# Two projections of a mixed attention and expert kernel: their inputs mixed once on ScalarE and VectorE instead of in the weights on TensorE

## The chip, the cores and the metric

One core of one Trainium2 chip runs the whole program. The metric is the device time of one execution in microseconds. Inside a core TensorE (PE), VectorE (DVE), ScalarE (ACT) and GpSimd (POOL) each run their own instruction list in order, and SyncE (SP) issues plain DMAs; they meet only at semaphores.

## The reference

x is 16 sequences of 512 tokens with 128 channels. After a layer norm, one branch is a recurrent attention with chunks of 32 tokens, the other a mixture of experts (8 experts, two per token, plus 8 small shared ones). The output is x + attention(x) * silu(experts(x)).

```python
xx = jnp.concatenate([jnp.zeros_like(x[:, :1]), x[:, :-1]], axis=1) - x
xk = x + xx * time_maa_k
xv = x + xx * time_maa_v
xr = x + xx * time_maa_r
r = split(proj(xr, Wr, br))
k = split(proj(xk, Wk, bk))
v = split(proj(xv, Wv, bv))
y, state = _wkv_chunked(r, k, v, time_decay, time_faaaa)
out = proj(y, Wo, bo)
...
routed = jnp.einsum('te,etd->td', gates, out_e)
alpha * shared + (1.0 - alpha) * routed
```

So each projection reads a mix of a token with the token in front of it: x*(1-m) + previous*m, with one m per channel.

## The kernel before

Values in float32 are held as a sum of two float16 numbers (high and low), and a product of two such values is three matmuls: high by high, high by low, low by high. The normed x lies transposed (channels on partitions) in `xh` and `xl`, with two zero columns ahead of each sequence, so that a slice shifted by one column is the previous token.

The program has four stages. First the norm, the transposes and the routing logits. Then a long run of expert work, which is 62 *units* cut in 206 *steps*: 12 shared units ahead of the sorted tokens (steps 0 to 47), then routed units with 4 shared ones mixed in. A wide unit (a shared one, or 512 sorted tokens) has 4 steps, a narrow one (256 sorted tokens) has 2. Steps 48 to 51 are two narrow units, 52 to 167 wide ones, 168 to 205 narrow ones. Last comes the recurrence over 16 pieces u, which this text calls the end stage.

One step i is a chain over the engines:

- PE, `pe_up(i)`: six 128x512 matmuls (twelve half ones for a narrow unit) into two of four PSUM banks; it waits for `gated` of step i-2. Then, in some steps, `pe_sorted` transposes a gathered block of 256 tokens, and `pe_down(i - 3)` makes the 12 small matmuls of an earlier step (LAG is 3; the profile's lines L1575 to L1577).
- ACT, `act_up(i)`, L781: silu of the first bank.
- DVE, `dve_up(i)`, L1218: its product with the second bank, called the gate here.
- ACT, `act_split(i)`, L785: the high half of that product.
- DVE, `dve_split(i)`, L1222: the low half. `pe_down(i)` needs both.

On DVE the list is gate(i), [the low half of a sorted block, L1211], low(i), [other work], gate(i+1). On ACT it is silu(i), [sorted block, L777], [a part, L817], high(i), [a copy out of PSUM when a unit ends, L805 or L807], silu(i+1). For wide units that copy falls on steps whose number leaves 2 when divided by 4, as every second sorted block does.

Between the steps r and k are projected in 32 *parts* of 512 tokens, one every 4 steps from step 75 (`PART_STEP`) to step 199. `pe_part` (L1596) stands at the end of step 75 + 4n: the mix is folded in the weights, W*(1-m) against x and W*m against the previous token, so a part is two times three matmuls of 512 columns. `act_part` adds the bias one step later (L817), `dve_part` makes the decayed copy two steps later (L1232), and SP stores both in DRAM. Parts 0 to 15 are r, 16 to 31 are k.

POOL gathers the sorted tokens (`pool_sorted`, L634, two indirect DMAs for each of 71 blocks, into `srows`, a ring of `NXB` blocks) and scatters the results (`pool_scatter`, L644, two for each block). Its list after the first seven blocks is strictly gather q, scatter q - 7, and a scatter waits for `y_out` of the block's unit. The end stage starts when all scatters have landed.

DVE also makes masks and weights for the end stage at ten even steps from `LATE_STEP` on, between gate and low half.

## Time and profile before

| what | value |
|---|---|
| median of the runs, us | 722.61 |
| lowest of the runs, us | 722.04 |
| span of the profiled execution, us | 719.3 |
| time around the span (median less span), us | 3.3 |
| silu of step 0, of step 74, of step 202, at us | 42.8, 229.4, 538.4 |
| first gather issued, at us | 154.7 |
| last scatter issued, at us | 554.0 |

The profiled execution's own total is not recorded apart from its span; the 3.3 us beside it are the median less the span, and they are added to every span below. Stage times are read from where the silu of a step starts. A length in the timeline is that of one instruction with its latency: on DVE and ACT the next one starts a little before the end of the one in front of it.

### The profile page before, as it was taken

To read this page: it belongs to the slowest core of one execution; us is meant where nothing else is said; L and a number is where in the kernel's file an instruction comes from. 1 tells how busy PE (TensorE), PEld (TensorE's weight loads), DVE (VectorE), ACT (ScalarE), POOL (GpSimd) and SP (SyncE) were. 2 spreads that over 40 slices of the span, in tenths; PEclk is the share of its full clock that TensorE was granted. 3 is DMA by queue.
4 is the path that set the end of the run, shared out by engine and by line. 5 is a ranking of instruction groups with operands and counts; after the bars stand their busy time and mean duration, and the time that the engine had idled before them with its cause. 6 is when DMAs were issued, how large, how long until landed. Compare 5 with 4: busy or idle time off the path is not lost.

```text
span 719.3 us, 22370 instructions
## 1 busy us (share of the span) xinstructions
PE 654.1 (91%) x8536; PEld 452.1 (63%) x8536; DVE 555.4 (77%) x1058; ACT 494.9 (69%) x1008; POOL 478.9 (67%) x519
## 2 busy tenths in 40 slices
PE   2787897978999999999999999999997899999993
PEld 1544565646665665566666666878886676777772
DVE  5989986877667886667766676667664899999996
ACT  4864798857665656666666666666665788888872
POOL 4844321244777777777777777767778487888873
PEclk9999999999999999999999999999999999999997
DMA  9931111111111323433323334333362767777762
GB/s 243 299 95 45 45 61 46 45 51 36 48 49 49 108 91 108 137 108 108 110 92 109 106 106 139 110 101 108 97 103 93 237 179 230 216 229 222 233 176 59
DMA packets 88616, 86.75 MB, mean 121 GB/s; under 512 B 11394, under 2 KB 65284, under 8 KB 88516
## 3 DMA queue, kind: packets, MB, share of 16 engines
q1 hardware_dynamic: 79428, 66.70, 29.8%
q0 software_dynamic: 9088, 18.63, 9.6%
q8 instruction: 73, 1.20, 0.7%
q14 instruction: 27, 0.22, 0.1%
HBM read 50.82 MB, written 34.47 MB: 119 GB/s over the span
## 4 chain that ended last, share of the span: by engine, by line
PE 53%; DVE 13%; ACT 12%; POOL 11%; issue 7%; DMA 3%; SPq 0%; POOLq 0%; DVEq 0%; ACTq 0%
PE banks L1556 7%; PE banks L1558 7%; PE banks L1557 7%; PE banks L1596 5%; DVE hidden L1218 4%; POOL expert_rows L644 4%; PE banks L1576 4%; PE banks L1577 4%; PE banks L1575 4%; POOL srows L634 3%; ACT hidden L785 3%; PE banks L1621 3%; PE banks L1693 3%; PE banks L1672 3%; ACT rows L823 2%
## 5 line engine op out<-in xcount | busy, mean ns | idle before, releaser
L785 ACT CAST hidden<-hidden 128x512 f16<-128x512 f32 x206 | 127.1, 617 | 135.5 <-DVE hidden L1218 135.4
L634 POOL DMA_INDIRECT srows<-normed_rows,source x142 | 149.7, 1054 | 60.4 <-issue 40.2
L1222 DVE TENSOR_TENSOR hidden<-hidden 128x512 f16<-128x512 f32 x180 | 124.4, 691 | 83.9 <-ACT hidden L785 83.0
L1218 DVE TENSOR_TENSOR hidden<-hidden,banks 128x512 f32<-128x512 f32 x206 | 140.8, 684 | 44.0 <-ACT hidden L781 38.2
L1575 PE MATMUL banks<-wwords,hidden 128*128 (+1 forms) x824 | 148.8, 219 | 1.5 <-DVE hidden L1222 1.1
L1576 PE MATMUL banks<-wwords,hidden 128*128 (+1 forms) x824 | 148.6, 219 | 0.0
L1577 PE MATMUL banks<-wwords,hidden 128*128 (+1 forms) x824 | 148.6, 219 | 0.0
L781 ACT ACTIVATE hidden<-banks 128x512 f32<-128x512 f32 x206 | 122.7, 596 | 28.1 <-PE banks L1558 27.8
L1556 PE MATMUL banks<-sx,wwords 128*128 128x512 f16 (+1 forms) x368 | 121.5, 330 | 3.2 <-DVE wwords L1013 2.7
L1558 PE MATMUL banks<-sx,wwords 128*128 128x512 f16 (+1 forms) x368 | 121.6, 330 | 0.0
L1557 PE MATMUL banks<-sx,wwords 128*128 128x512 f16 (+1 forms) x368 | 121.5, 330 | 0.0
L644 POOL DMA_INDIRECT expert_rows<-ybuf,dest x72 | 77.2, 1072 | 22.8 <-issue 19.8
L1575 PEld LDWEIGHTS banks<-wwords,hidden 128*128 128x128 f16 x824 | 80.6, 98 | 12.4 <-issue 2.0
L644 POOL DMA_INDIRECT expert_rows<-rows,dest x70 | 72.8, 1040 | 23.1 <-issue 20.1
L1576 PEld LDWEIGHTS banks<-wwords,hidden 128*128 128x128 f16 x824 | 80.6, 98 | 11.3
L624 POOL TENSOR_TENSOR hidden<-hidden 128x512 f16<-128x512 f32 x26 | 33.6, 1294 | 76.8 <-ACT hidden L785 76.8
L1303 DVE TENSOR_TENSOR wwords<-banks,wmat 128x1024 f32<-128x1024 f32 x64 | 75.3, 1217 | 10.9 <-PE banks L1672 10.5
L1577 PEld LDWEIGHTS banks<-wwords,hidden 128*128 128x128 f16 x824 | 80.6, 98 | 0.0
L1556 PE MATMUL banks<-xh,wwords 128*128 128x512 f16 x128 | 49.2, 385 | 19.1 <-DVE hidden L1218 18.7
L1321 DVE SCALAR_TENSOR_TENSOR hidden<-banks,cst,hidden 128x256 f32<-128x256 f32 x128 | 61.5, 481 | 3.8 <-ACT hidden L849 0.7
L1558 PEld LDWEIGHTS banks<-sx,wwords 128*128 x368 | 36.0, 98 | 25.6
L1557 PE MATMUL banks<-xl,wwords 128*128 128x512 f16 x128 | 49.0, 383 | 0.0
(218 smaller groups left out, 1429.7 us busy)
## 6 DMA issues: line engine op xcount, KB each, us to landing
rows<-x SPq DMA_DIRECT2D x32, 256.0 KB, 4.9
rows<-expert_rows SPq DMA_DIRECT2D x32, 256.0 KB, 3.6
normed_rows<-rows SPq DMA_DIRECT2D x16, 256.0 KB, 3.9
r_rows<-rows SPq DMA_DIRECT2D x16, 256.0 KB, 2.1
rd_rows<-rows SPq DMA_DIRECT2D x16, 256.0 KB, 2.2
stage<-r_rows SPq DMA_DIRECT2D x16, 256.0 KB, 4.0
k_rows<-rows SPq DMA_DIRECT2D x16, 256.0 KB, 2.2
kd_rows<-rows SPq DMA_DIRECT2D x16, 256.0 KB, 2.2
```

The lines of the kernel that those rows point to most:

```text
L634: G.indirect_dma_start(srows[:, q % NXB, t, :], None, rows_in, bass.IndirectOffsetOnAxis(source[:, at:at + 1], 0)).then_inc(sem[f"s_in{q % ...
L644: G.indirect_dma_start(rows_out, bass.IndirectOffsetOnAxis(dest[:, at:at + 1], 0), ring_of(q)[:, t, :], None).then_inc(sem[f"y_stored{q % ...
L781: A.activation(sg[:, i % 2, :], psum[2 * (i % 2)][:, :], ACT.Silu, scale=1.0 / SW).then_inc(sem["silu"], 1)
L785: A.copy(guh[:, i % 4, :], gu[:, i % 2, :]).then_inc(sem["gu_hi"], 1)
L1218: V.tensor_tensor(gu[:, i % 2, :], sg[:, i % 2, :], psum[2 * (i % 2) + 1][:, :], ALU.mult).then_inc(sem["gated"], 1)
L1222: V.tensor_tensor(gul[:, i % 4, :], gu[:, i % 2, :], guh[:, i % 4, :], ALU.subtract).then_inc(sem["gu_lo"], 1)
L1556: T.matmul(o, a, mh, start=True, stop=False)
L1557: T.matmul(o, a, ml, start=False, stop=False)
L1558: k = T.matmul(o, b, mh, start=False, stop=True)
L1575: T.matmul(o, guh[:, i % 4, s], a, start=(j == 0 and n == 0), stop=False)
L1576: T.matmul(o, guh[:, i % 4, s], b, start=False, stop=False)
L1577: k = T.matmul(o, gul[:, i % 4, s], a, start=False, stop=last)
```

## The change

`act_previous` (ACT, two steps ahead of the part) writes previous*m into `mixed`, `dve_mix` (DVE, the same step) adds x*(1-m), `act_mix_high` and `dve_mix_low` (one step ahead of the part) split it in two float16 tiles, and `pe_part` makes three products of 512 columns with unmixed weights, after a wait for `mix_lo`. `dve_xsum` (DVE, three steps ahead of every second part) adds `xh` and `xl` for 129 columns of four sequences; it serves the r part and the k part of the same tokens, which are now neighbours (n even is r, n odd is k). `mixed`, `mix_hi` and `mix_lo` are single tiles in `stage`. The work at `LATE_STEP` moves from steps 72 to 90 to steps 50 to 68, and the ring `srows` has five blocks. The weights of v and of the output keep their form, with new numbers. POOL's clearing of the first state now waits for the last part, and SP loads the first pieces of k at the last-but-one part.

```diff
@@ -152,7 +152,7 @@
-        NXB = 3
+        NXB = 5
         srows = sb("srows", [P, NXB, TPU, P])
...
@@ -245,6 +246,10 @@
         ypair = take([P, 2, TPU, P])
+
+        take = carve(stage[:, :, :].rearrange("p a b -> p (a b)"))
+        mixed = take([P, 512])
+        mix_hi, mix_lo = [take([P, 512], F16) for i in range(2)]
...
@@ -411,8 +416,8 @@
-        LATE_STEP = 72
-        R_PARTS, PARTS = NA, 2 * NA
+        LATE_STEP = 50
+        PARTS = 2 * NA
         PART_STEP = 75
...
@@ -645,6 +650,7 @@
             def pool_state0():
+                G.wait_ge(sem["part"], PARTS)
                 G.wait_ge(sem["w_hi"], 3 * (EXPERTS + 1))
...
@@ -815,6 +821,22 @@
+
+            def act_previous(n):
+                u, proj = divmod(n, 2)
+                A.wait_ge(sem["xsum"], u + 1)
+                if n == 0:
+                    A.wait_ge(sem["w_lo"], 3 * (EXPERTS + 1))
+                    A.wait_ge(sem["mix_in"], 48)
+                else:
+                    A.wait_ge(sem["mix_lo"], n)
+                A.mul(mixed[:, :].rearrange("p (b i) -> p b i", b=4), xsum[:, :, 0:P], mx[:, proj:proj + 1]).then_inc(sem["mix_prev"], 1)
+
+            def act_mix_high(n):
+                A.wait_ge(sem["mixed"], n + 1)
+                if n >= 1:
+                    A.wait_ge(sem["part"], n)
+                A.copy(mix_hi[:, :], mixed[:, :]).then_inc(sem["mix_hi"], 1)
...
@@ -913,6 +935,10 @@
                     act_split(i)
+                    if part_at(i + 2) is not None:
+                        act_previous(part_at(i + 2))
+                    if part_at(i + 1) is not None:
+                        act_mix_high(part_at(i + 1))
                     if y is not None and filled:
...
@@ -1222,16 +1247,39 @@
-                w = wb if n < R_PARTS else wk
+                w = (wb, wk)[n % 2]
-                    V.wait_ge(sem["mixes"], 7)
+                    V.wait_ge(sem["mixes"], 6)
+
+            def dve_xsum(u):
+                tt, g = where(u)
+                if u == 0:
+                    V.wait_ge(sem["x_lo"], nb)
+                    V.wait_ge(sem["zero_cols"], 2 * nb)
+                h, l = [a[:, 4 * g * XS:4 * (g + 1) * XS].rearrange("p (b s) -> p b s", s=XS)[:, :, 1 + tt * P:2 + (tt + 1) * P]
+                        for a in (xh, xl)]
+                V.tensor_tensor(xsum[:, :, :], h, l, ALU.add).then_inc(sem["xsum"], 1)
+
+            def dve_mix(n):
+                proj = n % 2
+                V.wait_ge(sem["mix_prev"], n + 1)
+                if n == 0:
+                    V.wait_ge(sem["mixes"], 1)
+                m = mixed[:, :].rearrange("p (b i) -> p b i", b=4)
+                V.scalar_tensor_tensor(m, xsum[:, :, 1:P + 1], omx[:, proj:proj + 1], m, ALU.mult, ALU.add).then_inc(sem["mixed"], 1)
+
+            def dve_mix_low(n):
+                V.wait_ge(sem["mix_hi"], n + 1)
+                if n >= 1:
+                    V.wait_ge(sem["part"], n)
+                V.tensor_tensor(mix_lo[:, :], mixed[:, :], mix_hi[:, :], ALU.subtract).then_inc(sem["mix_lo"], 1)
...
@@ -1249,32 +1297,34 @@
                     V.wait_ge(sem["mixes"], 1)
-                    V.tensor_scalar(ws32[:, 6, :], w32[:, 3, :], SW, None, ALU.mult).then_inc(sem["aconst"], 1)
-                V.tensor_scalar(ws32[:, i, :], w32[:, i, :], omx[:, i:i + 1], SW, ALU.mult, ALU.mult).then_inc(sem["aconst"], 1)
-                V.tensor_scalar(ws32[:, 3 + i, :], w32[:, i, :], mx[:, i:i + 1], SW, ALU.mult, ALU.mult).then_inc(sem["aconst"], 1)
+                    V.tensor_scalar(ws32[:, 1, :], w32[:, 1, :], SW, None, ALU.mult).then_inc(sem["aconst"], 1)
+                    V.tensor_scalar(ws32[:, 4, :], w32[:, 3, :], SW, None, ALU.mult).then_inc(sem["aconst"], 1)
+                else:
+                    V.tensor_scalar(ws32[:, 2, :], w32[:, 2, :], omx[:, 2:3], SW, ALU.mult, ALU.mult).then_inc(sem["aconst"], 1)
+                    V.tensor_scalar(ws32[:, 3, :], w32[:, 2, :], mx[:, 2:3], SW, ALU.mult, ALU.mult).then_inc(sem["aconst"], 1)
-                V.wait_ge(sem["aconst"], 8 + 2 * step)
-                for some in (slice(1, 3), slice(4, 7)):
-                    if step == 0:
-                        V.tensor_copy(wph[:, some, :], ws32[:, some, :]).then_inc(sem["aconst"], 1)
-                    else:
-                        V.tensor_tensor(wpl[:, some, :], ws32[:, some, :], wph[:, some, :], ALU.subtract).then_inc(sem["aconst"], 1)
+                V.wait_ge(sem["aconst"], 7 + step)
+                some = slice(1, 5)
+                if step == 0:
+                    V.tensor_copy(wph[:, some, :], ws32[:, some, :]).then_inc(sem["aconst"], 1)
+                else:
+                    V.tensor_tensor(wpl[:, some, :], ws32[:, some, :], wph[:, some, :], ALU.subtract).then_inc(sem["aconst"], 1)
...
@@ -1579,23 +1635,17 @@
             def pe_part(n):
-                u, proj = n % R_PARTS, n // R_PARTS
-                tt, g = where(u)
+                proj = n % 2
+                T.wait_ge(sem["mix_lo"], n + 1)
                 if n == 0:
-                    T.wait_ge(sem["mixes"], 6)
-                    T.wait_ge(sem["zero_cols"], 2 * nb)
                     T.wait_ge(sem["source"], 1)
                     T.wait_ge(sem["part_out"], n)
-                if n == R_PARTS:
-                    T.wait_ge(sem["aconst"], 12)
-                i = 0
-                for shift in range(2):
-                    mh, ml = [cols(t, g, shift)(tt) for t in (xh, xl)]
-                    for a, m in ((wph, mh), (wph, ml), (wpl, mh)):
-                        j = T.matmul(psum[7], a[:, 3 * shift + proj, :], m, start=(i == 0), stop=(i == 5))
-                        i += 1
-                j.then_inc(sem["part"], 1)
+                if n == 1:
+                    T.wait_ge(sem["aconst"], 9)
+                T.matmul(psum[7], wph[:, proj, :], mix_hi[:, :], start=True, stop=False)
+                T.matmul(psum[7], wph[:, proj, :], mix_lo[:, :], start=False, stop=False)
+                T.matmul(psum[7], wpl[:, proj, :], mix_hi[:, :], start=False, stop=True).then_inc(sem["part"], 1)
...
@@ -1618,7 +1668,7 @@
                         for a, m in ((ch, wph), (ch, wpl), (cl, wph)):
-                            j = T.matmul(o, a, m[:, 3 * shift + 2, :], start=False, stop=(n == 5))
+                            j = T.matmul(o, a, m[:, 2 + shift, :], start=False, stop=(n == 5))
                             n += 1
```

On DVE, in the third stage over the four steps from one whose number leaves 2 when divided by 4 (step 134 and its like): before,

```order
L1218 TENSOR_TENSOR hidden<-hidden,banks 128x512 [waits gu_lo,silu]
L1211 TENSOR_TENSOR sx<-banks,sx 128x256 [waits s_hi]
L1222 TENSOR_TENSOR hidden<-hidden 128x512 [waits gu_hi]
L1218 TENSOR_TENSOR hidden<-hidden,banks 128x512 [waits gu_lo,silu]
L1222 TENSOR_TENSOR hidden<-hidden 128x512 [waits gu_hi]
L1218 TENSOR_TENSOR hidden<-hidden,banks 128x512 [waits gu_lo,silu]
L1222 TENSOR_TENSOR hidden<-hidden 128x512 [waits gu_hi]
L1218 TENSOR_TENSOR hidden<-hidden,banks 128x512 [waits gu_lo,silu]
L1222 TENSOR_TENSOR hidden<-hidden 128x512 [waits gu_hi]
L1232 TENSOR_TENSOR rows<-rows,wb 128x512 [waits part_stored1,part_out]
```

and with the change (L1243 is the gate, L1247 the low half, L1282 `dve_mix_low`, L1268 `dve_xsum`, L1276 `dve_mix`, with `dve_part` next in the list):

```order
L1243 TENSOR_TENSOR hidden<-hidden,banks 128x512 [waits gu_lo,silu]
L1236 TENSOR_TENSOR sx<-banks,sx 128x256 [waits s_hi]
L1247 TENSOR_TENSOR hidden<-hidden 128x512 [waits gu_hi]
L1282 TENSOR_TENSOR stage<-stage 128x512 [waits part,mix_hi]
L1243 TENSOR_TENSOR hidden<-hidden,banks 128x512 [waits gu_lo,silu]
L1247 TENSOR_TENSOR hidden<-hidden 128x512 [waits gu_hi]
L1243 TENSOR_TENSOR hidden<-hidden,banks 128x512 [waits gu_lo,silu]
L1247 TENSOR_TENSOR hidden<-hidden 128x512 [waits gu_hi]
L1268 TENSOR_TENSOR xsum<-xh,xl 128x516
L1243 TENSOR_TENSOR hidden<-hidden,banks 128x512 [waits gu_lo,silu]
L1247 TENSOR_TENSOR hidden<-hidden 128x512 [waits gu_hi]
L1276 SCALAR_TENSOR_TENSOR stage<-xsum,omx,stage 128x512 [waits mix_prev]
```

The three new instructions all stand behind a low half and ahead of the next gate.

On ACT, two steps ahead of a part and one step ahead: before,

```order
L785 CAST hidden<-hidden 128x512 [waits gated]
L781 ACTIVATE hidden<-banks 128x512 [waits up]
L777 CAST sx<-banks 128x256 [waits s_flipped]
L785 CAST hidden<-hidden 128x512 [waits gated]
L805 COPY rows<-banks 128x512 [waits y_stored3,y_stored2,down]
L781 ACTIVATE hidden<-banks 128x512 [waits up]
L785 CAST hidden<-hidden 128x512 [waits gated]
```

and with the change (L787 is the silu, L791 the high half, L811 the copy of a finished unit, L833 `act_previous`, L839 `act_mix_high`):

```order
L791 CAST hidden<-hidden 128x512 [waits gated]
L833 ACTIVATE stage<-xsum,mx 128x512 [waits mix_lo,xsum]
L787 ACTIVATE hidden<-banks 128x512 [waits up]
L783 CAST sx<-banks 128x256 [waits s_flipped]
L791 CAST hidden<-hidden 128x512 [waits gated]
L839 CAST stage<-stage 128x512 [waits part,mixed]
L811 COPY rows<-banks 128x512 [waits y_stored3,y_stored2,down]
L787 ACTIVATE hidden<-banks 128x512 [waits up]
L791 CAST hidden<-hidden 128x512 [waits gated]
```

Both new instructions stand behind a high half and ahead of the next silu, the second of them also ahead of the copy.

On PE, at the end of a part's step and the start of the next: before,

```order
L1576 MATMUL banks<-wwords,hidden 128x128
L1577 MATMUL banks<-wwords,hidden 128x128
L1596 MATMUL banks<-xh,wph 128x512 [waits part_out]
L1596 MATMUL banks<-xl,wph 128x512
L1596 MATMUL banks<-xh,wpl 128x512
L1596 MATMUL banks<-xh,wph 128x512
L1596 MATMUL banks<-xl,wph 128x512
L1596 MATMUL banks<-xh,wpl 128x512
L1556 ISA [waits gated,s_lo]
L1556 MATMUL banks<-sx,wwords 128x512
```

and with the change (L1646 to L1648 are `pe_part`):

```order
L1632 MATMUL banks<-wwords,hidden 128x128
L1633 MATMUL banks<-wwords,hidden 128x128
L1646 MATMUL banks<-stage,wph 128x512 [waits part_out,mix_lo]
L1647 MATMUL banks<-stage,wph 128x512
L1648 MATMUL banks<-stage,wpl 128x512
L1612 ISA [waits gated,s_lo]
L1612 MATMUL banks<-sx,wwords 128x512
```

The part has half its products, and its first one now waits for DVE's `mix_lo`; the up matmuls of the next step are queued behind it.

## Rows read from the trace of the kernel before

**Rows 1.** Part 1 of the page: busy time of each engine.

```profile
PE 654.1 (91%) x8536; PEld 452.1 (63%) x8536; DVE 555.4 (77%) x1058; ACT 494.9 (69%) x1008; POOL 478.9 (67%) x519
```

**Rows 2.** Windows view (columns: stretch, busy per engine, PEclk, DMA share, GB/s).

```profile
213.00:290.00 77.00, 74.36 (x642) 47.01 (x641) 57.81 (x104) 48.00 (x92) 60.13 (x56) 1.00 0.27 86
290.00:540.00 250.00, 249.08 (x2334) 177.02 (x2332) 171.22 (x280) 161.87 (x313) 189.71 (x182) 1.00 0.36 110
```

**Rows 3.** Chain that ended last, by line, in the stretch 340 to 380 us.

```profile
by line: PE banks L1556 17.8%; PE banks L1557 17.8%; PE banks L1558 17.3%; PE banks L1596 16.5%; PE banks L1577 8.9%; PE banks L1576 8.9%; PE banks L1575 8.9%; PE banks L1509 4.4%
```

**Rows 4.** Groups by line, POOL, 290 to 540 us (busy, mean ns, idle before, releasers).

```profile
L634 POOL DMA_INDIRECT srows<-normed_rows,source x89 | 92.1, 1035 | 30.3 <-issue 25.9 <-PE banks L1509 4.4
L644 POOL DMA_INDIRECT expert_rows<-ybuf,dest x47 | 49.9, 1062 | 15.2 <-issue 12.8 <-ACT ybuf L805 1.2 <-ACT rows L807 0.9
L644 POOL DMA_INDIRECT expert_rows<-rows,dest x46 | 48.3, 1050 | 14.9 <-issue 13.1 <-ACT rows L805 1.2 <-ACT ybuf L805 0.3
```

**Rows 5.** Timeline of POOL: the longest wait after 290 us, the next gather.

```profile
471.16 1.31 POOL L634 DMA_INDIRECT srows<-normed_rows,source  x1 [3.53 <-PE banks L1509]
472.77 0.96 POOL L634 DMA_INDIRECT srows<-normed_rows,source  x1 [0.30 <-issue]
```

**Rows 6.** Timeline of DVE over one period (start, length, line, idle before).

```profile
367.16 0.68 DVE L1218 TENSOR_TENSOR hidden<-hidden,banks 128x512 f32<-128x512 f32 x1
...
368.52 0.69 DVE L1222 TENSOR_TENSOR hidden<-hidden 128x512 f16<-128x512 f32 x1 [0.35 <-ACT hidden L785]
369.51 0.69 DVE L1218 TENSOR_TENSOR hidden<-hidden,banks 128x512 f32<-128x512 f32 x1 [0.29 <-ACT hidden L781]
...
372.01 0.69 DVE L1218 TENSOR_TENSOR hidden<-hidden,banks 128x512 f32<-128x512 f32 x1 [0.44 <-ACT hidden L781]
...
374.19 0.69 DVE L1218 TENSOR_TENSOR hidden<-hidden,banks 128x512 f32<-128x512 f32 x1
375.56 0.69 DVE L1222 TENSOR_TENSOR hidden<-hidden 128x512 f16<-128x512 f32 x1 [0.69 <-ACT hidden L785]
376.17 0.69 DVE L1232 TENSOR_TENSOR rows<-rows,wb 128x512 f32<-128x512 f32 x1
376.77 0.68 DVE L1218 TENSOR_TENSOR hidden<-hidden,banks 128x512 f32<-128x512 f32 x1
```

**Rows 7.** Timeline of ACT, step 130 to 131.

```profile
367.87 0.62 ACT L785 CAST hidden<-hidden 128x512 f16<-128x512 f32 x1 [1.10 <-DVE hidden L1218]
368.40 0.58 ACT L805 COPY rows<-banks 128x512 f32<-128x512 f32 x1
368.87 0.60 ACT L781 ACTIVATE hidden<-banks 128x512 f32<-128x512 f32 x1
```

**Rows 8.** Timeline of PE: first product of part 14, last of up(132).

```profile
368.57 0.38 PE L1596 MATMUL banks<-xh,wph 128*128 128x512 f16 x1
...
370.96 0.38 PE L1558 MATMUL banks<-sx,wwords 128*128 128x512 f16 x1
```

**Rows 9.** Timeline of DVE around the first mask of the third stage.

```profile
225.82 0.68 DVE L1218 TENSOR_TENSOR hidden<-hidden,banks 128x512 f32<-128x512 f32 x1
226.41 1.22 DVE L1240 TENSOR_TENSOR wmat<-wmat,cst 128x1024 f32<-128x1024 f32 x1
227.55 0.68 DVE L1222 TENSOR_TENSOR hidden<-hidden 128x512 f16<-128x512 f32 x1
```

**Rows 10.** Timeline of ACT: the silu of step 74 and of step 202.

```profile
229.39 0.59 ACT L781 ACTIVATE hidden<-banks 128x512 f32<-128x512 f32 x1
...
538.41 0.60 ACT L781 ACTIVATE hidden<-banks 128x512 f32<-128x512 f32 x1
```

**Rows 11.** Timeline of ACT and POOL: last copy of expert rows, last scatter.

```profile
548.88 0.37 ACT L807 COPY rows<-banks 128x256 f32<-128x256 f32 x1 [1.54 <-PE banks L1577]
...
554.04 0.97 POOL L644 DMA_INDIRECT expert_rows<-rows,dest  x1 [0.31 <-issue]
```

**Rows 12.** Windows view, a stretch of the first eleven units.

```profile
100.00:120.00 20.00, 16.38 (x155) 10.52 (x153) 13.83 (x22) 18.85 (x32) 4.50 (x4) 0.96 0.14 47
```

60 lines of the change are left out of this document (33 added, 27 removed).

## The prediction

> **What bounds the kernel now.** I read the page's busy shares first: PE is busy 91% of the span and no other engine over 77% [rows 1], which suggests PE, but is a mean over four stages. So next the windows of the routed stretch. From 213 to 290 us PE is busy 74.4 of 77 us and from 290 to 540 us 249.1 of 250 at full clock [rows 2]. The chain of waits agrees: between 340 and 380 us it consists of PE lines alone, and 16.5% of it is the part, L1596 [rows 3]. There a matmul taken away is time taken away, as long as nobody else is close behind.
>
> Two others are. POOL shows 189.7 us busy in the same 250 us [rows 2], but each of its 182 issues is followed by some 0.30 us that the profile calls issue; what it truly waited for is 4.4 us on PE and 1.2 + 0.9 + 1.2 + 0.3 = 3.6 us on ACT [rows 4], and the largest of these is a single wait of 3.53 us [rows 5]. So POOL could run this stretch at most 8.0 us faster.
>
> The other is the loop between DVE and ACT, and it shows only in the timeline. In step 130 the gate starts at 367.16, the low half at 368.52; in step 133 they are at 374.19 and 375.56 [rows 6]. The 1.37 us between them are the gate, then ACT's high half, which starts 0.71 after the gate (367.87) [rows 7]. DVE stands idle for half of it, but its list is in order, so nothing behind the low half can use that hole. Behind a low half the next instruction starts 0.61 later (375.56 to 376.17) and one more costs 0.60 (376.17 to 376.77) [rows 6]. The shortest step of this loop is therefore 1.36 + 0.61 = 1.97 us. The period of four steps 130 to 133 took 376.77 - 367.16 = 9.61 us; the loop alone would need 4 x 1.97, 0.60 for the decayed copy and 0.38 for step 130, where the copy of a finished unit holds the silu (gate 131 at 369.51 and not at 369.13; ACT's starts are 367.87, 368.40, 368.87) [rows 6, 7]: 8.9 us. It has 0.7 us of slack in 9.6, and that is all the room there is for the new work.
>
> **PE's side.** The last product of up(132) starts 2.39 us after the first of part 14, eleven products later: 0.217 us each [rows 8]. Three fewer save 0.65 us a part, 32 x 0.65 = 20.8 us in all if PE stays last.
>
> **DVE's and ACT's side.** The new instructions have no row of their own. The nearest for the three on DVE is the decayed copy, of the same 128x512 in float32: 0.60 to the next start and 0.69 long [rows 6]. A wide instruction there can cost nothing if it falls in the hole and 0.69 if nothing overlaps; I take 0.61, since all three stand behind a low half. I walk the period again from gate 130 at 367.16.
>
> Step 130 (one ahead of the part). Low half 368.52, `dve_mix_low` 369.13. Its input, ACT's `act_mix_high`, starts 0.53 behind the high half, at 368.40, and is like it 0.62 us long [rows 7], so it is there by 369.02. `dve_mix_low` ends at 369.82. The part on PE started at 368.57 [rows 8]; it now waits until about 369.92, with 0.10 for the semaphore and the weights (between 0 and 0.2). The copy of the finished unit moves to 368.93, silu 131 to 369.40, gate 131, 0.64 behind its silu [rows 6, 7], to 370.04.
>
> Step 131 and the start of 132. Queued behind the waiting part on PE are the up matmuls of step 132; behind those wait ACT's silu and DVE's gate. From the part's first product to gate 132 it is 372.01 - 368.57 = 3.44 us now [rows 6, 8], less 0.65 with three products: gate 132 at 369.92 + 2.79 = 372.71. DVE itself would be free at 370.04 + 1.97 = 372.01. The two gates are 5.55 us apart and were 4.85.
>
> Step 132. It took 2.18 us (372.01 to 374.19) [rows 6]. DVE's `dve_xsum`, every second time, makes it 1.97 + 0.61 = 2.58; the mean is 2.38.
>
> Step 133 (two ahead of the next part). It took 2.58 [rows 6]. `act_previous` starts 0.53 behind the high half, 1.24 after the gate, and is done, at ACT's lengths of 0.60 to 0.62 [rows 7], about when DVE comes to `dve_mix`, 1.97 after the gate. That adds 0.61: 3.19.
>
> Sum: 5.55 + 2.38 + 3.19 = **11.12 us a period** against 9.61, 1.5 us more although PE does less. Between the silus of steps 74 and 202 there are 32 periods in 538.41 - 229.39 = 309.0 us [rows 10], 9.66 each. Now 32 x 11.12 = 355.8: **46.8 us more**. POOL needs (309.0 - 8.0)/32 = 9.4 us a period on average and stays ahead of this loop.
>
> On the price of one more instruction the Trainium skill, "VectorE: DVE Perf Modes", section "The DRAIN you can't avoid", speaks otherwise: the next instruction starts only when the pipeline is empty. By it each of the 2.5 new ones in a period would cost its full 0.69 and not 0.61, some 6 us more in the sum. The trace shows 0.60 between the starts of an instruction of 0.69 and the next [rows 6], so the row is kept.
>
> **The smaller parts.** The late work moves to steps 50 to 68, into DVE's hole there. A mask makes the way from gate to low half 227.55 - 225.82 = 1.73 instead of 1.37, 0.36 more [rows 9]; beside a sorted block it also loses the room of that. For ten such steps I bound it by 0 (POOL's list may be what is late there) and 10 x 0.5 = 5, and take 2. The gain where the work leaves is nothing, since POOL held that stretch too. The ring of five: a gather no longer waits for the third block before it, but the scatter next in POOL's list waits for its unit all the same, so I take 0, between 0 and the 4.4 us of rows 4 as a gain. At the end of the stretch POOL was late: ACT's last copy of expert rows started at 548.88, the last scatter at 554.04 [rows 11]. With POOL caught up only two scatters come behind that copy, at about 549.3 and 550.6, 3.4 us sooner; I take 2, as the first loads of the end stage hide some of it. POOL's new wait for the last part is long over by then, and SP issues its later loads of k ten steps before the end stage; both cost nothing, and a few us if that cover were gone. The weights of v and the output keep their number of products.
>
> Together 719.3 + 46.8 + 2 - 2 = 766.1 us of span, and with the 3.3 us around it **769.4 us**.
>
> **Rivals.** *The part does not wait.* If PE comes late enough, or DVE early enough, that `mix_lo` is there, gate 132 is at 372.01, the period 4.85 + 2.38 + 3.19 = 10.42, and the whole 26 us slower: 748.6. For it speaks only that my 0.7 us is a difference of two estimates. *POOL becomes the bound.* If the new DVE and ACT work finds room in their waits (DVE is busy 171 of 250 us, ACT 162 [rows 2]), PE saves 0.65 a part and POOL stops the gain at 8.0 us: 714.6, no change that can be told. The in-order lists speak against it. *PE's saving is whole.* As before, and the longer ring lets POOL run ahead: 722.6 - 20.8 = 701.8, faster. It needs DVE's loop to grow by less than 0.05 us a period (8.9 + x below 9.61 - 0.65), while 2.5 new instructions stand in it, and POOL to do in 12.8 us less than its issues allow. *The clock falls.* From 100 to 120 us PE was busy 16.4 of 20 us, having waited for DVE and ACT, and the granted clock was 0.96 on average, so between the levels of 2.4 and 1.2 GHz [rows 12]; with the change PE waits about 2 us in each 11. If 8% of the time were at the lower level, the nine products of a period's late path (2.0 us) would take 0.16 longer: 5 us, 774.5. The Trainium skill, "TensorE: Matmul & The Clock Gate", section "The HAM clock gate", says that the gate follows how busy the array has been of late, which agrees in direction.
>
> **How the numbers follow.** A difference of 2%, 14.5 us, is about what a measurement of this kernel tells from none. I give my forecast 0.62, the part that does not wait 0.13, the clock or otherwise longer instructions 0.10, POOL as bound 0.12, the whole saving 0.03. Leaving out the last two and a few hundredths of the tails, the range is 741 to 780. Faster by over 2%: 0.04; within 2%: 0.13; slower: 0.83.
>
> **What would show it.** In the timeline of the changed kernel: gates of a period 5.5, 2.0 or 2.6, and 3.2 us apart; each part's first product right behind the end of `dve_mix_low`, with PE idle ahead of it for over 1 us; POOL's waits for PE and ACT grown from 8 to some 50 us; PE no longer the engine of the chain from 230 to 540 us, but DVE and ACT with it. I would be wrong if DVE ran any new instruction in its hole, if a new one took well under 0.6 us, or if PE stayed over 95% busy in that stretch.

## The result

| what | before | after |
|---|---|---|
| median of the runs, us | 722.33 | 794.80 |
| range of the runs beside it, us | 720.6 to 722.6 | 792.6 to 796.2 |
| span of the profiled execution, us | 719.3 | 790.6 |
| silu of step 0, of step 74, of step 202, at us | 42.8, 229.4, 538.4 | 44.6, 233.6, 610.7 |
| mean granted TensorE clock | 0.988 | 0.954 |

The changed kernel takes 1.1005 times as long, with a 95% interval of 1.0977 to 1.1033: 72 us more for three matmuls less in each of 32 parts. One execution of the kernel before took 2308 us and is left out of the range. The forecast was 769.4 us in a range of 741 to 780. The direction and the longer loop were right; the size was not, because the sum put the price of TensorE's clock at nothing.

Where the time went can be read from four marks. Step 0 starts 1.8 us later. That is no part of the change: the same code up to there starts step 0 at 43.0 in the first experiment below. From step 0 to step 74 it is 189.0 us and was 186.6, 2.4 more. From step 74 to step 202 it is 377.2 us and was 309.0 [rows 10]: **68.2 us more**. From step 202 to the end it is 179.9 and was 180.9. So nearly everything lies in the stretch with the parts.

Part 1 of the page after, which answers to [rows 1]:

```profile
PE 662.0 (84%) x8440; PEld 456.0 (58%) x8440; DVE 604.5 (76%) x1134; ACT 526.3 (67%) x1072; POOL 474.5 (60%) x519
```

96 matmuls are gone, and still PE is busy 7.9 us longer. A matmul count that falls while the busy time rises means that single matmuls took longer, and that points at the clock. The windows of the changed kernel, as in [rows 2] (columns: stretch, its length, busy time of PE, PEld, DVE, ACT, POOL, granted clock, DMA share, GB/s):

```profile
213.00:290.00 77.00, 64.99 (x567) 41.25 (x565) 57.11 (x97) 48.85 (x94) 55.55 (x54) 1.00 0.24 77
290.00:540.00 250.00, 206.10 (x1712) 135.06 (x1711) 169.69 (x277) 151.12 (x288) 154.91 (x152) 0.93 0.28 88
```

PE was busy 249.1 of 250 us here and is now busy 206.1, for fewer steps, and the granted clock has gone from 1.00 to 0.93. Who waits for whom stands in the view of waits (who waits for whom: us in total, times, longest):

```profile
PE banks L1646 <- DVE stage L1282: 66.2, 32, 2.7
DVE hidden L1243 <- ACT hidden L787: 65.3, 82, 4.3
ACT hidden L787 <- PE banks L1614: 54.9, 57, 2.6
```

All 32 parts wait for `dve_mix_low` (L1282), 2.07 us each on average. L1243 is the gate now, L787 the silu, L791 the high half, L1247 the low half, L1612 to L1614 the up matmuls. The second and third row are one and the same delay handed on: the up matmuls stand behind the waiting part, ACT waits for them, and DVE for ACT. POOL, by line from 290 to 540 us, answers to [rows 4]:

```profile
L639 POOL DMA_INDIRECT srows<-normed_rows,source x76 | 77.0, 1014 | 25.9 <-issue 20.4 <-PE banks L1565 5.5
L649 POOL DMA_INDIRECT expert_rows<-rows,dest x40 | 41.8, 1044 | 36.3 <-ACT rows L811 26.5 <-issue 9.7
L649 POOL DMA_INDIRECT expert_rows<-ybuf,dest x36 | 36.8, 1023 | 33.2 <-ACT ybuf L811 24.2 <-issue 8.9
```

It truly waited 5.5 + 26.5 + 24.2 = 56.2 us here and 8.0 before, so it does not bound the changed kernel. The chain of 340 to 380 us, PE lines alone before [rows 3], now runs over every engine of the loop (its end is cut by the view itself):

```profile
by line: issue 14.0%; ACT hidden L791 12.1%; DVE hidden L1243 9.4%; PE banks L1614 7.6%; PE banks L1613 7.3%; DVE stage L1282 6.9%; PE banks L1612 6.5%; DVE hidden L1247 5.7%; DVE rows L1257 5.1%; PE banks L1646 3.9%; DVE xsum L1268 3.4%; A
```

**One period at full clock.** The timeline of DVE, steps 134 to 137 (start, length, line, idle before):

```profile
409.76 0.68 DVE L1243 TENSOR_TENSOR hidden<-hidden,banks 128x512 f32<-128x512 f32 x1
410.36 0.41 DVE L1236 TENSOR_TENSOR sx<-banks,sx 128x256 f16<-128x256 f32 x1
411.12 0.69 DVE L1247 TENSOR_TENSOR hidden<-hidden 128x512 f16<-128x512 f32 x1 [0.35 <-ACT hidden L791]
411.73 0.68 DVE L1282 TENSOR_TENSOR stage<-stage 128x512 f16<-128x512 f32 x1
412.63 0.69 DVE L1243 TENSOR_TENSOR hidden<-hidden,banks 128x512 f32<-128x512 f32 x1 [0.21 <-ACT hidden L787]
414.00 0.69 DVE L1247 TENSOR_TENSOR hidden<-hidden 128x512 f16<-128x512 f32 x1 [0.69 <-ACT hidden L791]
415.26 0.69 DVE L1243 TENSOR_TENSOR hidden<-hidden,banks 128x512 f32<-128x512 f32 x1 [0.57 <-ACT hidden L787]
...
417.24 0.69 DVE L1268 TENSOR_TENSOR xsum<-xh,xl 128x516 f32<-128x516 f16 x1
417.85 0.68 DVE L1243 TENSOR_TENSOR hidden<-hidden,banks 128x512 f32<-128x512 f32 x1
419.21 0.69 DVE L1247 TENSOR_TENSOR hidden<-hidden 128x512 f16<-128x512 f32 x1 [0.69 <-ACT hidden L791]
419.83 0.75 DVE L1276 SCALAR_TENSOR_TENSOR stage<-xsum,omx,stage 128x512 f32<-128x512 f32 x1
420.50 0.68 DVE L1257 TENSOR_TENSOR rows<-rows,wk 128x512 f32<-128x512 f32 x1
421.11 0.68 DVE L1243 TENSOR_TENSOR hidden<-hidden,banks 128x512 f32<-128x512 f32 x1
```

The gates are 415.26 - 409.76 = 5.50, then 2.59 and 3.26 us apart, 11.35 together; this is a period with `dve_xsum`, for which the prediction's terms are 5.55 + 2.58 + 3.19 = 11.32. The three new instructions stand where the prediction put them, and DVE's hole of 0.69 between gate and low half is still empty.

**One period with a fallen clock.** The period before, 397.14 to 409.76, took 12.62 though it has no `dve_xsum`. The timeline of PE shows why. The last down matmul ahead of the part started at 397.41:

```profile
399.85 0.39 PE L1646 MATMUL banks<-stage,wph 128*128 128x512 f16 x1 [2.23 <-DVE stage L1282]
400.08 0.38 PE L1647 MATMUL banks<-stage,wph 128*128 128x512 f16 x1
400.30 0.38 PE L1648 MATMUL banks<-stage,wpl 128*128 128x512 f16 x1
400.51 0.44 PE L1612 MATMUL banks<-sx,wwords 128*128 128x512 f16 x1
400.75 0.63 PE L1613 MATMUL banks<-sx,wwords 128*128 128x512 f16 x1
401.17 0.63 PE L1614 MATMUL banks<-sx,wwords 128*128 128x512 f16 x1
401.60 0.63 PE L1612 MATMUL banks<-sx,wwords 128*128 128x512 f16 x1
402.03 0.63 PE L1613 MATMUL banks<-sx,wwords 128*128 128x512 f16 x1
```

The part's products start 0.22 us apart, as at 2.4 GHz. After an idle of 2.23 us and three to four products the pitch becomes 0.43: the level of 1.2 GHz, until about 404.1. The windows view has half the clock there:

```profile
400.80:404.00 3.20, 3.20 (x15) 1.84 (x14) 0.94 (x2) 1.42 (x4) 2.34 (x3) 0.50 0.15 46
```

These are the up matmuls that the whole loop is waiting for. What one such spell costs is read from pairs of periods, each with one `dve_xsum`. The first products of the parts start at 237.08, 259.38, 281.67, 304.00, every second one, and these pairs are 22.3 us long; from there they start at 327.96, 351.92, 375.89, 399.85, 423.82, 447.79, 471.76, 23.96 us long: 1.65 us for a spell. From 304 on, every second part has a spell, 13 in all: 13 x 1.65 = 21.5 us. Over time the spell begins earlier against its part: in the sixth product from the part's first at 304.00, in the fourth at 399.85, the third at 519.75, the first at 591.74. At 495.74, 543.70, 567.73 and 591.74 it falls on the half-size products of narrow steps, 0.21 us apart in place of 0.11. (The narrow steps are 164 to 171 and 176 to 205, with a wide shared unit at 172 to 175, and not 168 to 205 as said ahead of the prediction; the pairs there are 24.0 us long, and 22.3 with the clock held up in the first experiment below, as the wide ones are.) The six parts ahead of 304 have none, with the same idle of 1.8 and 2.2 us ahead of them.

### The profile page after: what moved, and what is told of

Read it like the earlier page. It is cut to its first block, busy times and chain, and to the rows that moved or that the text cites. A ratio compares the mean times of both kernels' runs of the same rounds, so it can differ in the third digit from the quotient of the medians.

```text
span 790.6 us, 22444 instructions
## 1 busy us (share of the span) xinstructions
PE 662.0 (84%) x8440; PEld 456.0 (58%) x8440; DVE 604.5 (76%) x1134; ACT 526.3 (67%) x1072; POOL 474.5 (60%) x519
## 4 chain that ended last, share of the span: by engine, by line
DVE 30%; PE 30%; ACT 21%; issue 13%; POOL 3%; DMA 1%; DVEq 0%; SPq 0%; POOLq 0%; ACTq 0%
DVE hidden L1243 11%; ACT hidden L791 10%; DVE hidden L1247 4%; ACT hidden L787 4%; PE banks L1614 3%; PE banks L1613 3%; PE banks L1612 3%; PE banks L1671 3%; DVE stage L1282 3%; DVE rows L1257 3%; PE banks L1722 3%; PE banks L1743 2%; ACT rows L845 2%; PE banks L1646 2%; POOL hidden L676 2%
## 5 line engine op out<-in xcount | busy, mean ns | idle before, releaser
L791 ACT CAST hidden<-hidden 128x512 f16<-128x512 f32 x206 | 127.1, 617 | 151.9 <-DVE hidden L1243 151.9
L1243 DVE TENSOR_TENSOR hidden<-hidden,banks 128x512 f32<-128x512 f32 x206 | 140.7, 683 | 66.5 <-ACT hidden L787 65.3
L1247 DVE TENSOR_TENSOR hidden<-hidden 128x512 f16<-128x512 f32 x180 | 124.5, 692 | 85.0 <-ACT hidden L791 84.2
L639 POOL DMA_INDIRECT srows<-normed_rows,source x142 | 147.5, 1038 | 54.2 <-issue 38.1
L787 ACT ACTIVATE hidden<-banks 128x512 f32<-128x512 f32 x206 | 121.9, 592 | 55.0 <-PE banks L1614 54.9
L1631 PE MATMUL banks<-wwords,hidden 128*128 (+1 forms) x824 | 152.6, 222 | 1.5 <-DVE hidden L1247 1.1
L1632 PE MATMUL banks<-wwords,hidden 128*128 (+1 forms) x824 | 152.0, 222 | 0.0
L1633 PE MATMUL banks<-wwords,hidden 128*128 (+1 forms) x824 | 151.6, 222 | 0.0
L1612 PE MATMUL banks<-sx,wwords 128*128 128x512 f16 (+1 forms) x368 | 126.1, 343 | 4.4 <-DVE wwords L1038 2.7
L1614 PE MATMUL banks<-sx,wwords 128*128 128x512 f16 (+1 forms) x368 | 126.8, 345 | 0.0
L1613 PE MATMUL banks<-sx,wwords 128*128 128x512 f16 (+1 forms) x368 | 126.6, 344 | 0.0
L649 POOL DMA_INDIRECT expert_rows<-ybuf,dest x72 | 74.5, 1034 | 66.9 <-ACT ybuf L811 25.2
L1631 PEld LDWEIGHTS banks<-wwords,hidden 128*128 128x128 f16 x824 | 82.3, 100 | 12.6 <-issue 2.2
L1632 PEld LDWEIGHTS banks<-wwords,hidden 128*128 128x128 f16 x824 | 82.1, 100 | 11.9 <-issue 0.3
L1633 PEld LDWEIGHTS banks<-wwords,hidden 128*128 128x128 f16 x824 | 82.0, 99 | 0.0
L1646 PE MATMUL banks<-stage,wph 128*128 128x512 f16 x32 | 12.7, 395 | 66.2 <-DVE stage L1282 66.2
L1612 PE MATMUL banks<-xh,wwords 128*128 128x512 f16 x128 | 50.9, 398 | 18.7 <-DVE hidden L1243 18.3
L1614 PEld LDWEIGHTS banks<-sx,wwords 128*128 x368 | 37.4, 102 | 27.7 <-issue 2.2
```

What stands on the lines that cost most here:

```text
L639: G.indirect_dma_start(srows[:, q % NXB, t, :], None, rows_in, bass.IndirectOffsetOnAxis(source[:, at:at + 1], 0)).then_inc(sem[f"s_in{q % ...
L649: G.indirect_dma_start(rows_out, bass.IndirectOffsetOnAxis(dest[:, at:at + 1], 0), ring_of(q)[:, t, :], None).then_inc(sem[f"y_stored{q % ...
L787: A.activation(sg[:, i % 2, :], psum[2 * (i % 2)][:, :], ACT.Silu, scale=1.0 / SW).then_inc(sem["silu"], 1)
L791: A.copy(guh[:, i % 4, :], gu[:, i % 2, :]).then_inc(sem["gu_hi"], 1)
L1243: V.tensor_tensor(gu[:, i % 2, :], sg[:, i % 2, :], psum[2 * (i % 2) + 1][:, :], ALU.mult).then_inc(sem["gated"], 1)
L1247: V.tensor_tensor(gul[:, i % 4, :], gu[:, i % 2, :], guh[:, i % 4, :], ALU.subtract).then_inc(sem["gu_lo"], 1)
```

## The experiments

Each run stood beside runs of the kernel before on the same chip. Edits are against the changed kernel unless said otherwise.

### PE kept from idling: eight extra products

```diff
                 else:
                     T.wait_ge(sem["part_out"], n)
+                for j in range(8):
+                    T.matmul(psum[7], wph[:, 0, :], xh[:, j * XS + 2:j * XS + 2 + WIDE], start=(j == 0), stop=(j == 7))
+                T.wait_ge(sem["mix_lo"], n + 1)
```

The wait for `mix_lo`, first in `pe_part` until now, moves behind them; the part's own products overwrite the bank.

> The changed kernel, with eight extra products of 512 columns (8 x 0.217 = 1.74 us) on TensorE ahead of each part's wait for mix_lo. Their result is overwritten by the part. Theory (the wait on DVE's mix_lo costs twice, by itself and because TensorE's clock falls after it): the extra products fit in the wait of 1.8 to 2.7 us, the granted clock stays near 1.0 from 230 to 610 us, a period of four steps takes about 11.2 us and not 11.8, so 32 x 0.6 = 19 us less than the changed kernel: about 775 us. Rival (the clock is no cause, only the lists of DVE and ACT are): the same 794.8 us. Rival (TensorE's own work still bounds): 32 x 1.74 = 56 us more, 850 us.

Measured: 773.6 us (772.5 to 774.4), 1.071 times the kernel before (1.0685 to 1.0734). Doing 256 matmuls more made the kernel 21 us faster. The granted clock of 290 to 540 us is back at full:

```profile
290.00:540.00 250.00, 241.82 (x2031) 153.41 (x2029) 182.28 (x297) 161.68 (x309) 162.19 (x160) 1.00 0.30 93
```

The silus of steps 74 and 202 start here:

```profile
233.67 0.58 ACT L787 ACTIVATE hidden<-banks 128x512 f32<-128x512 f32 x1
...
589.35 0.60 ACT L787 ACTIVATE hidden<-banks 128x512 f32<-128x512 f32 x1
```

355.7 us or 11.11 a period. With the clock out of the way, the walk of the prediction (11.12, 355.8) holds, part's wait included. The whole is still 4.2 us above the forecast of 769.4; where these stand is told behind the experiments.

### Four extra products: busy share or idle stretch?

The same edit with 4 in place of 8. It leaves PE idle for part of the wait.

> e1_fill with four extra products (0.87 us) and not eight. TensorE still stands idle for 1.0 to 1.8 us ahead of each part. Theory (the clock falls after a long idle stretch, not because TensorE is less busy on the whole): the clock stays up in nearly all periods, about 774 us as with eight. Rival (it goes by the busy share alone): between the 795 us of the changed kernel and the 774 us of e1_fill, about 785 us.

Measured: 775.1 us (773.9 to 778.1), 1.0741 (1.0707 to 1.0776), so the same as with eight (1.0685 to 1.0734). One of its parts in the timeline of PE:

```profile
390.98 1.03 PE L1644 MATMUL banks<-xh,wph 128*128 128x512 f16 x4
393.37 0.39 PE L1648 MATMUL banks<-stage,wph 128*128 128x512 f16 x1 [1.36 <-DVE stage L1282]
393.59 0.38 PE L1649 MATMUL banks<-stage,wph 128*128 128x512 f16 x1
```

The idle time ahead of a part is 1.36 (three times 1.6 to 1.8) where it was 2.2 and 1.0 where it was 1.8, and no spell is left. It is enough to shorten the idle stretch; filling it brings nothing more. It does not tell idle stretch from busy share: four products also raise PE's busy time from 206.1 to 222.0 of the 250 us, and only the rival that the loss goes in proportion to the share (785) is ruled out.

### The same work one step earlier

```diff
-                    if part_at(i + 2) is not None:
-                        act_previous(part_at(i + 2))
-                    if part_at(i + 1) is not None:
-                        act_mix_high(part_at(i + 1))
+                    if part_at(i + 3) is not None:
+                        act_previous(part_at(i + 3))
+                    if part_at(i + 2) is not None:
+                        act_mix_high(part_at(i + 2))
```

and on DVE likewise `dve_xsum` at i + 4, `dve_mix` at i + 3, `dve_mix_low` at i + 2. The part finds `mix_lo` ready.

> The changed kernel, with the sum, the mix and the split made one step earlier against the part (four, three and two steps ahead, not three, two and one), at the same places behind a low half. Theory: the part no longer waits, the clock stays up, and what is left is DVE's in-order list: four shortest steps of 1.97, 0.38 for the copy, and 0.30 + 0.67 + 0.61 + 0.60 for sum, mix, low half and decayed copy, 10.4 us a period; 32 x (11.79 - 10.4) = 44 us less than the changed kernel: about 751 us. Rival (only the new instructions count, not the wait on the part): 795 us. Rival (only the wait counts): POOL is last, 714 us.

Measured: 746.6 us (746.4 to 747.6), 1.034 (1.0318 to 1.0362). Silu 74 starts at 232.91 and silu 202 at 563.36: 330.5 us, 10.33 a period. No row of waits for DVE stands ahead of a part any more:

```profile
337.24 0.38 PE L1646 MATMUL banks<-stage,wph 128*128 128x512 f16 x1
```

This is the first rival of the prediction (period 10.42, 748.6 us; by the rule of its main sum it would be 32 x 10.42 - 309.0 = 24.4 us more, 747.0) made to happen. Beside the run with eight extra products, the wait by itself, at full clock, is 773.6 - 746.6 = 27 us.

### The same work in the holes

On ACT the two instructions move from behind the high half to ahead of it, on DVE all of them, the decayed copy too, from behind the low half to between gate and low half.

```diff
+                if part_at(i + 7) is not None and part_at(i + 7) % 2 == 0:
+                    dve_xsum(part_at(i + 7) // 2)
+                if part_at(i + 4) is not None:
+                    dve_mix(part_at(i + 4))
+                if part_at(i + 2) is not None:
+                    dve_mix_low(part_at(i + 2))
+                if part_at(i - 3) is not None:
+                    dve_part(part_at(i - 3))
                 if not low_on_pool(i):
                     dve_split(i)
```

with the old places removed, ACT's at i + 4 and i + 2 ahead of `act_split`, and a wait of `dve_xsum` for the last reader of its tile.

> The changed kernel with the same instructions at other places of the lists: on ACT previous and high ahead of the high half of the step (four and two steps ahead of the part), on DVE mix and low of the mix ahead of the low half of the same steps, the sum seven steps ahead and the decayed copy three steps behind, also ahead of the low half. Theory (what costs is the place, behind a low half, not the instruction): the new work falls in the 0.76 us in which DVE waits for the high half, DVE's loop takes 4 x 1.97 + 0.38 + about 0.3 = 8.6 us a period, TensorE does not wait for mix_lo, and POOL is last: about 714 us. Rival (each of the new instructions costs its length wherever it stands): 750 us or more.

Measured: 726.4 us (721.5 to 728.0, 10 runs), 1.0046 (1.0024 to 1.0067). So 20 us of the 24 that the early version lost are recovered by the place; the forecast 714 was missed by 12. Two things moved with it: the lead over the part is one to three steps longer, which can bring little since no part of the early version waits, and the decayed copy, an old instruction of 0.60 us a period, left its place behind the low half too. What the new instructions alone would cost in the hole was not run. Silu 74 at 235.33, silu 202 at 541.97: 306.6 us, 9.58 a period with every new instruction in it. DVE's hole is used and costs nothing: with `dve_mix` (L1278) in it the low half starts 411.40 - 410.03 = 1.37 behind the gate, as without:

```profile
407.68 0.68 DVE L1243 TENSOR_TENSOR hidden<-hidden,banks 128x512 f32<-128x512 f32 x1
408.28 0.42 DVE L1236 TENSOR_TENSOR sx<-banks,sx 128x256 f16<-128x256 f32 x1
408.61 0.68 DVE L1257 TENSOR_TENSOR rows<-rows,wk 128x512 f32<-128x512 f32 x1
409.21 0.68 DVE L1247 TENSOR_TENSOR hidden<-hidden 128x512 f16<-128x512 f32 x1
410.03 0.69 DVE L1243 TENSOR_TENSOR hidden<-hidden,banks 128x512 f32<-128x512 f32 x1
410.64 0.75 DVE L1278 SCALAR_TENSOR_TENSOR stage<-xsum,omx,stage 128x512 f32<-128x512 f32 x1
411.40 0.69 DVE L1247 TENSOR_TENSOR hidden<-hidden 128x512 f16<-128x512 f32 x1
```

Only beside a sorted block does the low half slip, to 1.53 behind its gate (407.68 to 409.21). Why no gain is left is seen better with no mix at all.

### Three products and no mix at all

DVE's and ACT's new instructions are left out and the part multiplies x itself, so r and k are projections of x and not of the mix. It shows how much the saving on PE can bring in this kernel.

> The changed kernel with the mix left out altogether: three products of 512 columns of the unmixed tokens a part, no sum, mix or split on ACT and DVE, so r and k are projections of x alone. It measures TensorE's saving by itself. Theory: TensorE would save 32 x 0.65 = 20.8 us, but POOL's list has only some 8 us of slack: about 714 us. Rival (the saving is whole once the ring has five blocks): 702 us. Rival (the ring, the moved late work or the new order of r and k cost something by themselves): above 722 us.

Measured: 721.0 us (717.6 to 724.5, 9 runs), 0.998 (0.9956 to 1.0003): neither 714 nor 702. The chain of 290 to 540 us begins:

```profile
by line: POOL expert_rows L649 17.4%; POOL srows L639 15.5%; issue 13.3%; PE banks L1604 6.8%; PE banks L1602 6.8%; PE banks L1603 6.8%; DMA srows<-normed_rows,source 4.9%; DVE hidden L1239 3.7%; PE banks L1622 3.6%; PE banks L1621 3.6%; PE
```

POOL leads it, as the theory of POOL as bound says, but it gave back less than the 8.0 us. The timeline of POOL names the places where it waits for more than 0.5 us between its first gather and its last scatter, and those two:

```profile
156.77 1.36 POOL L639 DMA_INDIRECT srows<-normed_rows,source  x1 [5.73 <-DVE source L1195]
...
187.25 1.14 POOL L649 DMA_INDIRECT expert_rows<-ybuf,dest  x1 [4.88 <-ACT ybuf L813]
...
200.69 1.00 POOL L649 DMA_INDIRECT expert_rows<-rows,dest  x1 [2.54 <-ACT rows L811]
...
552.63 0.96 POOL L649 DMA_INDIRECT expert_rows<-rows,dest  x1 [0.30 <-issue]
```

(and two of 1.29 and 1.99 at 175.06 and 179.24). From 200.69 it never stops: 351.9 us to the last scatter. The kernel before, in the same view, has its last wait ahead of the parts at 197.52 and two more in the parts' stretch beside that of [rows 5]:

```profile
197.52 0.99 POOL L644 DMA_INDIRECT expert_rows<-rows,dest  x1 [1.18 <-ACT rows L805]
340.42 0.99 POOL L644 DMA_INDIRECT expert_rows<-ybuf,dest  x1 [1.18 <-ACT ybuf L805]
416.90 0.99 POOL L644 DMA_INDIRECT expert_rows<-rows,dest  x1 [1.18 <-ACT rows L805]
```

From 197.52 it took 554.04 - 197.52 = 356.5 us, with 1.18 + 1.18 + 3.53 = 5.9 us of waits in it. So 4.6 us were won behind that scatter, and it was issued 3.2 later: 2.1 because the whole program started later in this execution, 1.1 because the head of the list took longer. With the deeper ring POOL waits less for blocks there, and runs ahead to a scatter whose unit is not ready. The kernel before with the ring of five alone, its late work at step 72 as ever, has the same two waits:

```profile
186.18 1.05 POOL L644 DMA_INDIRECT expert_rows<-ybuf,dest  x1 [5.39 <-ACT ybuf L807]
...
198.85 0.99 POOL L644 DMA_INDIRECT expert_rows<-rows,dest  x1 [2.06 <-ACT rows L805]
```

and the changed kernel with a ring of three has only one of 1.18 there, as before the change. From first gather to last scatter the list takes 395.9 us with no mix, 400.1 with the mix in the holes, 399.4 before. Before, its 284 issues are 299.7 us long (1.06 each) with 80.1 of issue between them, 380 us, and 19.3 us of waits behind the first gather; with no mix the waits are 14.4, and the issues 1.4 longer. So what there was to win is small. That POOL is what holds the time is read from its timeline and the chain; no run made its list shorter by itself.

The profiled execution gained nothing of this in the end: its last scatter is 1.4 us earlier than before, and from there to the end it took 168.7 us and 165.3 before. That part of the program varies: it is 170.5 us in the trace of the kernel before with the ring of five, so no cause can be read from it.

### The ring, alone and undone

The kernel before with `NXB = 5`, and the changed kernel with `NXB = 3`.

> The kernel before with a ring of five blocks, on whichever chip the call falls. On a chip where the kernel before takes 722 us: theory, within 3 us of it; rival, 3 to 4% slower as on the two chips where the kernel before took 820 to 830 us.

> The changed kernel with NXB 3 in place of 5. Theory: POOL waits for 100 us in the changed kernel, its ring bounds nothing: within 3 us of the changed kernel's 795 us. Rival (the ring of five is part of the loss): faster by over 5 us.

Measured: 722.8 us, 1.0003 (0.9987 to 1.002), and 795.4 us, 1.1017 (1.0987 to 1.1047). The ring is neither part of the loss nor a gain: in the trace of the kernel before with five blocks POOL waited 3.9 us for blocks and 11.9 for units, with three 14.5 and 4.8.

### A longer lag for the scatters

The version with the work in the holes, with `LATE_STEP` 64 and scatter q - 9 in place of q - 7, so that POOL has gathers to issue while a unit is unfinished.

> The kernel of e9_lag9 (work in the holes, late work at step 64, scatter nine blocks behind the gather). Theory (POOL's list is last, 5 us of gathers moved into its first wait, late work off the first wide unit): 718 to 722 us where the kernel before takes 722 us and e4_holes 726. Rival: the 726 us of e4_holes.

Measured: 724.4 us (721.7 to 725.6, 10 runs), 1.0019 (1.0002 to 1.0037). Of the waits for units at the head of the list, 4.88 and 2.54 with q - 7, one of 1.18 is left. But the scatters to `expert_rows` from `ybuf` took 1.117 us each and 1.072 before, the gathers 1.075 and 1.054, and the list is 398.6 us long, as ever. Against the version with q - 7, which ran on another chip (1.0024 to 1.0067), the intervals overlap, so no gain is shown, and two things were changed at once. It is not better than the kernel before: the expectation was missed. On the chips where the kernel before takes 722 us, no version with the mix beat it.

### Two chips that tell little

The ring alone and three variants of the version in the holes (`LATE_STEP` 64; then scatter q - 8; then q - 9) first ran on another chip, and were repeated on a third.

> The kernel before with NXB 5 in place of 3 and nothing else. Theory: the second half of POOL's list is strictly gather, scatter, and a scatter waits for its unit, so a longer ring lets POOL ahead by two blocks once and then gives nothing: within 3 us of the 722.4 us of the kernel before. Rival (the ring was what held POOL): POOL's waits for transposes, 4.4 us after 290 us and 9.8 us before, go, and the time falls by 5 to 10 us.

> The kernel e4_holes with the late work at steps 64 to 82 in place of 50 to 68. In e4_holes POOL issues without a pause from 202.9 us (its scatter of the first wide unit, which waited 2.5 us for that unit) to 558 us. Theory: the late work on DVE at steps 50 to 58 delays that unit, and with it the whole list of POOL: 2 to 3.5 us less than e4_holes, about 723.5 us. Rival (its place does not matter, since POOL is last): 726.4 us.

> e7_late64 with scatter q - 8 and not q - 7 behind gather q: POOL issues one more block of gathers in the time in which it waits for the first units. Theory (POOL's list is what is last in the third stage): one block of gathers, 2 x 1.3 us, moves into that wait: 2.6 us less than e7_late64. Rival (POOL is last only because the units come at their pace): no difference, or more, since a copy out of PSUM waits longer for its place in the ring of four.

> The same with q - 9: two blocks of gathers in the wait. Theory: up to 2.6 us less than e8_lag8 as far as the ring of five has room; the ninth gather waits for the transpose of block 4, so it may be less. Rival: POOL's order comes to wait on TensorE and TensorE on POOL's scatters, and it is slower than e8_lag8.

And of the repetition:

> The kernel of e5_ring5 again (the kernel before with a ring of five blocks), since in that call the kernel before itself took 830 us, with pauses of up to 8 us on ACT and DVE that no engine ended. Theory: within 3 us of the kernel before. Rival: 5 to 10 us faster, or as in that call 3% slower.

> The kernel of e7_late64 again, for the same reason. Theory: 2 to 3.5 us less than e4_holes, so within 1 us of the kernel before where e4_holes was 0.5% above it. Rival: as e4_holes, 0.5% above.

> The kernel of e8_lag8 again. Theory (POOL's list is last): 2.6 us less than f2_late64. Rival: no less.

> The kernel of e9_lag9 again. Theory: up to 2.6 us less than f3_lag8, so 0.5 to 1% below the kernel before. Rival: no less, or slower by a new wait between POOL and TensorE.

On the first of these chips the kernel before itself took 830.1 us and the four 862.3, 851.5, 830.2 and 817.3; on the second it took 820.3, and they 848.1, 840.7, 819.9 and 810.0. The order is the same both times, with ratios of 1.03 to 1.04, 1.02 to 1.03, 1.00 and 0.98 to 0.99. But the traces there, which are of these versions and not of the kernel before, all have what none of the traces on the other chips has, ACT idle with nothing of this core that ends it:

```profile
ACT hidden L781 <- remote: 83.2, 20, 8.1
```

(the view of waits, ring alone, first of the two chips.) The longest such pause of a trace is 4.7 to 8.8 us. There the time falls with a longer lag, from 851.5 to 830.2 and 817.3; that it is because the longer lag bears the pauses better is likely, but not shown. On an undisturbed chip the ring alone is 1.0003 and not 1.03. Where the pauses come from is open.

## Why the prediction was right or wrong

**What bounds the kernel.** Right in kind: the loop between DVE and ACT had 0.7 us of slack, and the work put behind the low halves went past it. With no mix the time stays at 721.0, and with all the mix in the holes at 726.4, so it was neither the work nor PE that cost 72 us, but its place. The 72 us come apart in three: 21 for the fallen clock (794.8 to 773.6), 27 for the part's wait (to 746.6), 24 for the places behind the low halves (to 722.4, the kernel before).

**The walk of the period.** Right. Predicted 11.12 us on average, 11.11 measured once the clock was held up; the gates of a single period were predicted within 0.07 us. The terms that were off are small: `dve_mix` costs 0.67 to the next start and not 0.61 (419.83 to 420.50), `dve_xsum` 0.61 as assumed (417.24 to 417.85); behind `dve_mix_low` the next gate waits for ACT, so its price can't be read there. The 0.10 between the end of `dve_mix_low` and the part had no row; it is 0.07 (411.73 + 0.68 to 412.48). The part's wait was expected to be over 1 us and was 2.07.

**The failed step: the price of the falling clock.** The sum of 769.4 has no term for it. The mechanism stood among the rivals with the sum "5 us, 774.5" and a chance of 0.10. It began from a mean granted clock of 0.96 in a stretch of the first units, made 8% of the time out of it, and spread that evenly over a period, so that only 2.0 us of late path could be longer, by 0.16. The runs showed that the low level is not spread: it comes in one spell, in every second part, and falls on the up matmuls that follow the idle time, which are the late path. Measured it is 377.2 - 355.7 = 21.5 us with the clock fallen and held up, 0.67 a period, four times the price. In spans, 766.1 + 21.5 = 787.6, and with the 1.8 us by which the program started later, 789.4 against the measured 790.6. (The 3.3 us around the span were 1.3 too many: it is 2.0 in the profiled execution of the changed kernel, 792.6 - 790.6, and 1.9 to 2.2 in all others with both numbers.) The range ended at 780, so it had room for twice the 5 us and not for four times. A bound from above was at hand, the late path of 2.0 us at half speed in every period, 64 us, and nothing in the trace before excluded it. The Trainium skill, "TensorE: Matmul & The Clock Gate", section "The HAM clock gate", has the clock follow how busy the array has been; the run with four extra products agrees in direction, since four products ahead of the wait kept it at full. Why the falls begin at 304 us no run shows.

**The late work and the tail.** Step 0 to 74 grew by 2.4, of which 2 were predicted for the moved late work; what else stands in it was not told apart. From step 202 to the end it is 1.0 us shorter, 2 were predicted; that is less than two traces of the kernel before differ there, 180.9 and 183.6 us with three and five blocks, so it proves nothing. These two terms also make up why the run with eight extra products lies above 769.4: there they are 4.1 and +1.1 and not 2 and -2, with 1.3 less around the span.

**The ring.** Zero, as taken; the 4.4 us that were given as its most did not come, since POOL then waits for units in place of blocks.

**POOL as the bound.** Its condition was met in two runs, and its number, 714.6, was not: 721.0 and 726.4. The 8.0 us took every wait between 290 and 540 us for won. Over the whole list only 4.9 of 19.3 us of waits went, the issues themselves grew by 1.4, and the ring moved waits to its head.

**What would show it.** The four signs all came: in a period at full clock gates 5.5, 2.6 and 3.3 apart, parts right behind `dve_mix_low`, POOL's waits at 56 us, PE no longer alone in the chain.

## What to carry to other kernels

When work moves from a full engine to half-idle ones, look for the place in their in-order lists: the same instructions cost 24 us behind the low half and 4 us in the hole ahead of it (where the decayed copy moved with them), and a consumer placed one step too near cost another 27. When a change makes PE wait at one regular place, price the clock as a spell at half speed on whatever follows that wait, and not as a share of the whole. And look first whether the saving can be had at all: taking the new work out entirely showed that three matmuls less in each part bring nothing that can be told (0.9956 to 1.0003), and POOL's timeline says why: its list of 284 indirect DMAs is nearly as long as the stretch.

## What the runs showed of the hardware

An idle of 2.2 us in an otherwise busy PE was followed, after five products at full speed at first and within the first product at the last, by a spell at 1.2 GHz over the up matmuls and the first down matmuls behind them. The same idle, at the same spacing, was followed by none at 237, 259 and 281 us and by one in every second part from 304 us on. The idle of 1.8 us ahead of the parts between was followed by none, nor was that of 0.9 to 1.8 us with four extra products. So the length of the idle alone doesn't decide; what else does was not tried and stays open. Extra matmuls whose result nobody reads made a kernel 21 us faster.

Two of the chips ran the kernel before 14 and 15% slower than the others, and the traces taken there have pauses on ACT of up to 8.8 us that no engine of the trace ends.
